# The first two units of a graph layer in halves, with the end of the setup between their products

## The reference

```python
HW = einsum('bnf,fo->bno', layernorm(x), W)
A_norm = relu((A + A.T) * 0.5)
D = sum(A_norm, axis=1);  d = D ** -0.5 where D > 0, else 0
out = relu((eye(N) - d[:, None] * A_norm * d[None, :]) @ HW)
x = x + out
x = x + moe(layernorm(x))     # 8 experts, top 2, gelu(t @ w1 + b1) @ w2 + b2
```

## Time and profile before

| | us |
|---|---|
| median of three runs | 880.55 |
| profiled execution | 878.45 |
| its span, first to last instruction | 876.3 |
| TensorE busy | 840.2 (96%) |
| DVE, ACT, POOL busy | 638.6, 476.6, 325.3 |

### The profile page before, as it was taken

One profiled execution on the slowest core, in us unless ns is written; L12 is line 12 of the kernel. 1 busy time (PEld: TensorE's weight loads), 2 busy tenths in 40 slices (PEclk: granted clock), 3 DMA queues, 4 the chain that ended last, 5 costly groups with the idle time before them and its releaser, 6 DMA issues.

```text
span 876.3 us, 14318 instructions
## 1 busy us (share of the span) xinstructions
PE 840.2 (96%) x4098; PEld 698.8 (80%) x4098; DVE 638.6 (73%) x1558; ACT 476.6 (54%) x871; POOL 325.3 (37%) x319
## 2 busy tenths in 40 slices
PE   3688999999999999999999999999999999999998
PEld 3577788888888888888888787788888888888886
DVE  3688644578889654442516499999999999999997
ACT  2687423233334200121111488888888888888886
POOL 1893253564757545455445539101000000000000
PEclk9996999999999999999999999999999999999999
DMA  9994376686766257977778866777877777777772
GB/s 282 330 318 142 120 276 253 228 288 237 267 210 211 90 178 285 327 269 263 258 277 313 307 247 231 271 286 284 296 272 266 262 265 281 275 288 292 286 267 80
DMA packets 93472, 223.00 MB, mean 254 GB/s; under 512 B 8904, under 2 KB 60128, under 8 KB 81520
## 3 DMA queue, kind: packets, MB, share of 16 engines
q1 hardware_dynamic: 88304, 213.23, 68.5%
q0 software_dynamic: 2608, 8.33, 2.4%
q10 hardware_dynamic: 2512, 0.86, 0.4%
HBM read 157.89 MB, written 64.49 MB: 254 GB/s over the span
## 4 chain that ended last, share of the span: by engine, by line
PE 90%; DVE 3%; ACT 3%; issue 2%; DMA 1%; POOL 1%; DVEq 0%; ACTq 0%; POOLq 0%
PE bank L959 13%; PE bank L961 13%; PE bank L960 13%; PE bank L1408 6%; PE bank L1392 6%; PE bank L1394 6%; PE bank L1405 6%; PE bank L1393 6%; PE bank L1406 6%; PE bank L344 3%; PE bank L448 2%; PE bank L896 2%; PE bank L1414 1%; PE bank L325 1%; ACT s_tri L607 1%
## 5 line engine op out<-in xcount | busy, mean ns | idle before, releaser
L1450 ACT ACTIVATE act_h<-bank,b_sb 128x512 f32<-128x512 f32 x256 | 176.9, 691 | 46.2 <-PE bank L1394 37.3
L1492 DVE TENSOR_TENSOR gated<-c_all,act_h 128x512 f32<-128x512 f32 x256 | 177.8, 695 | 25.1 <-ACT act_h L1450 19.7
L1497 DVE TENSOR_TENSOR g_lo<-gated,g_hi 128x512 fp32r<-128x512 f32 x256 | 175.7, 686 | 0.2
L1457 ACT ACTIVATE g_hi<-gated 128x512 fp32r<-128x512 f32 x256 | 159.6, 623 | 6.1 <-DVE gated L1492 6.0
L1368 POOL DMA_DIRECT2D out<-fin x31 | 23.7, 763 | 308.3 <-DVE fin L1505 308.3
L1030 POOL TENSOR_SCALAR z<-x,mv,rstd 128x128 f32<-128x128 f32 x128 | 107.6, 853 | 3.4
L959 PE MATMUL bank<-y_hi,stage 128*128 128x512 f32 x256 | 105.7, 413 | 1.3 <-DVE y_lo L734 0.7
L981 ACT ACTIVATE z_hl<-bank 128x512 fp32r<-128x512 f32 x32 | 19.2, 599 | 155.2 <-PE bank L896 155.2
L1392 PE MATMUL bank<-z_e,w_hi 128*128 128x512 f32 x256 | 102.7, 401 | 0.1
L1408 PE MATMUL bank<-g_lo,w_hi 128*128 128x512 f32 x256 | 100.9, 394 | 1.1 <-DVE g_lo L1497 1.0
L961 PE MATMUL bank<-y_hi,stage 128*128 128x512 f32 x256 | 101.3, 396 | 0.0
(11 more groups left out here) (133 smaller groups left out, 1487.8 us busy)
## 6 DMA issues: line engine op xcount, KB each, us to landing
c_all<-c_scratch SPq DMA_DIRECT2D x64, 1024.0 KB, 8.0
s_scratch<-stage SPq DMA_DIRECT2D x14, 2048.0 KB, 8.2
stage<-s_scratch SPq DMA_DIRECT2D x14, 2048.0 KB, 7.9
z_e<-z_scratch SPq DMA_DIRECT2D x32, 512.0 KB, 7.3
z_scratch<-z_hl SPq DMA_DIRECT2D x31, 512.0 KB, 2.7
x_raw<-in_x SPq DMA_DIRECT2D x32, 256.0 KB, 6.4
x_res<-in_x SPq DMA_DIRECT2D x32, 256.0 KB, 7.2
r_e<-res_scratch SPq DMA_DIRECT2D x32, 256.0 KB, 2.7
```

What stands on the lines that cost most here:

```text
L1450: act.activation(v.act_h[e % R][:, :], ps_h[e % 2][:, :], ACT.Gelu, bias=v.b1_sb[:, e:e + 1]).then_inc(gelu_done, 1)
L1457: act.activation(v.g_hi[e % R][:, :], v.gated[e % R][:, :], ACT.Copy).then_inc(hi_done, 1)
L1492: dve.tensor_tensor(out=v.gated[e % R][:, :], in0=v.c_all[s][:, e, :], in1=v.act_h[e % R][:, :], op=ALU.mult).then_inc(gated_done, 1)
L1497: dve.tensor_tensor(out=v.g_lo[e % R][:, :], in0=v.gated[e % R][:, :], in1=v.g_hi[e % R][:, :].bitcast(FP32), op=ALU.subtract).then_inc(lo ...
```

## The change

Units 0 and 1 are each multiplied in two parts: blocks 15 to 8 of unit 0, the same of unit 1, blocks 7 to 0 of unit 0, the same of unit 1. d comes in two parts (8 to 15, 0 to 7). Rows 3 to 0 of adj (the 13th to 16th) are transposed between the products of the first part and leave the loop over the rows. x blocks 8 to 11 go with the 8th to 11th row, and x blocks 12 to 15 are loaded behind all rows and worked on between products; two new x buffers lie where Y will be. Two groups of unit 0's S are made behind the sixth and seventh row, its direct blocks behind the eleventh. Groups of S are counted from the top block down, and products wait for the part of S that they need. The sums of the last rows use two PSUM banks instead of three. turn_z and route of units 0 and 1, and the stores of these units, move to units 2 and 3.

```diff
-    PARTS = [(8, 16), (3, 8), (0, 3)]
+    PARTS = [(8, 16), (0, 8)]
-    LAST = 6
-    FIRST_AT = {15: (0, 1), 14: (2, 3)}
-    SECOND_AT = (7, 5, 3, 0)
-    JOBS = [2, 2, 2, 2, 1, 1, 1, 1, 1, 1, 1, 1, 0, 0, 0, 0]
+    LAST = 9
+    ROWS_APART = 12
+    JOBS = [2, 2, 2, 2, 0, 0, 0, 1, 1, 1, 1, 0, 0, 0, 0, 0]
...
+        for k in range(EARLY, MB):
+            pr.load(sp, k)
...
 # scalar (ACT)
+        for r, j in enumerate(ROWS[:ROWS_APART]):
             for k in jobs(r):
                 pr.copy_x(act, k)
             for g in range(n_groups(j)):
                 relu(r, j, g)
+            for k in [k - 1 for k in jobs(r) if k] if r < 4 else [7] if r == 4 else [r] if r >= 8 else []:
+                pr.keep(act, k)
+            if r in (5, 6):
+                st.high_group(act, 0, r - 5)
+            if r == 10:
+                st.high_direct(act, 0)
+                y_high(15)
+                y_high(14)
+        y_high(13)
+        y_high(12)
+        relu(12, 3, 0)
+        y_high(11)
+        relu(13, 2, 0)
+        y_high(10)
+        relu(14, 1, 0)
+        y_high(9)
+        relu(15, 0, 0)
+        st.high_direct(act, 1)
+        st.high_group(act, 1, 0)
+        y_high(8)
+        st.high_group(act, 1, 1)
+        pr.copy_x(act, 12)
+        act.wait_ge(pr.xt_turned, EARLY)
+        act.wait_ge(pr.x_mv_done, EARLY)
+        st.high_group(act, 0, 2)
+        y_high(7)
+        pr.keep(act, 12)
+        pr.copy_x(act, 13)
+        y_high(6)
+        st.high_group(act, 1, 2)
+        pr.keep(act, 13)
+        pr.copy_x(act, 14)
+        y_high(5)
+        y_high(4)
+        st.high_group(act, 0, 3)
+        pr.keep(act, 14)
+        pr.copy_x(act, 15)
+        y_high(3)
+        st.high_group(act, 1, 3)
+        pr.keep(act, 15)
+        y_high(2)
+        y_high(1)
+        y_high(0)
...
 # vector (DVE)
+            if r in (5, 6):
+                st.low_group(dve, 0, r - 5)
+            if r == 8:
+                degrees(0)
+                for u in range(2):
+                    st.diagonal(dve, u)
             if r == 9:
+                add_columns(8)
+            if r == 10:
+                st.low_direct(dve, 0)
+                y_low(15)
+                y_low(14)
+        y_low(13)
+        y_low(12)
+        add_columns(7)
+        add(12, 3, 0)
+        y_low(11)
+        add_columns(6)
+        add(13, 2, 0)
+        y_low(10)
+        add_columns(5)
+        add(14, 1, 0)
+        y_low(9)
+        add_columns(4)
+        add(15, 0, 0)
+        st.low_direct(dve, 1)
+        st.low_group(dve, 1, 0)
+        y_low(8)
+        add_columns(3)
+        add_columns(2)
+        add_columns(1)
+        st.low_group(dve, 1, 1)
+        pr.statistics(dve, 12)
+        degrees(1)
+        st.low_group(dve, 0, 2)
+        y_low(7)
...
 # tensor, in the setup
+            if r in (4, 11):
+                pr.project(pe, 7 if r == 4 else 11)
             for g in range(n_groups(j)):
                 turn(r, j, g)
+            if r == 5:
+                st.turn_group(pe, 0, 0)
+            if r == 6:
+                st.turn_group(pe, 0, 1)
...
 # tensor, units 0 and 1
+        def after_first(u, m):
+            if u == 0 and m >= 8:
+                if m == 14:
+                    v.turn_last(12, 3, 0)
+                if m == 12:
+                    v.turn_last(13, 2, 0)
+                if m == 11:
+                    v.turn_last(14, 1, 0)
+                    st.turn_group(pe, 1, 0)
+                    st.turn_group(pe, 1, 1)
+                if m == 10:
+                    v.turn_last(15, 0, 0)
+            elif m >= 8:
+                if m == 15:
+                    pr.turn_x(pe, 12)
+                if m == 13:
+                    for k in range(7, -1, -1):
+                        v.column_sum(k)
+                if m == 12:
+                    pr.project(pe, 12)
+                    pr.turn_x(pe, 13)
+                if m == 11:
+                    st.turn_group(pe, 0, 2)
+                if m == 10:
+                    pr.project(pe, 13)
+                    pr.turn_x(pe, 14)
+                if m == 9:
+                    st.turn_group(pe, 1, 2)
+            elif u == 0:
+                if m == 7:
+                    pr.project(pe, 14)
+                    pr.turn_x(pe, 15)
+                if m == 6:
+                    st.turn_group(pe, 0, 3)
+                if m == 5:
+                    pr.project(pe, 15)
+                if m == 4:
+                    st.turn_group(pe, 1, 3)
+            else:
+                if m == 5:
+                    st.turn_group(pe, 2, 0)
+                    st.turn_group(pe, 2, 1)
+                if m == 2:
+                    st.turn_group(pe, 2, 2)
+                    st.turn_group(pe, 2, 3)
+        for part in range(4):
+            u = part % 2
+            for m in range(MB - 1, 7, -1) if part < 2 else range(7, -1, -1):
+                if u == 0:
+                    pe.wait_ge(v.y_lo_done, MB - m)
+                pe.wait_ge(st.lo_made, st.ops_for(u, m))
+                products(u, m, u, acc[u], MB - 1 - m)
+                after_first(u, m)
```

More of the change, by code:

```diff
@@ L442, in turn_group @@
     def turn_group(pe, u, g):
[L443 removed]
+        n, G = column(u), turn_index(u, g)
+        a, b = blocks(u, g)
         if G >= 2:
[L445 to L447 removed]
+            pe.wait_ge(lo_made, ops_with(*part_turned[G - 2]))
+        for m in range(a, b):
+            i = m - a
             last = pe.transpose(ps_t[G % 2][:, i * P:(i + 1) * P], v.s_tri[:, block(n, m), :], v.ident[:, :])
@@ L590, in gpsimd @@
                 add_columns(j)
-            if r == 10:
+            if r == 9:
                 root(0)
-            if r == 14:
-                root(1)
-        root(2)
+        pr.invert(pool, [EARLY])
+        root(1)
+        for k in range(EARLY + 1, MB):
+            pr.invert(pool, [k])
     def scalar(act):
@@ L834, in graph_stage @@
     each_router, each_rest = diagonal[:, :, 0:E], diagonal[:, :, E:2 * E]
+    LATE = [[], [], [0], [1, 2]] + [[u - 1] for u in range(4, U)]
     def landed(eng, sems, u):
@@ L930, in between @@
             if i == 12:
-                if u:
+                if u > 2:
                     turn_z(u - 1)
-                for g in groups[2:4] if u else ():
+                for g in groups[2:4]:
                     st.turn_group(pe, u + 1, g)
-            if u > 1 and i == ROUTE_AT:
+            if u > 3 and i == ROUTE_AT:
                 route(u - 2)
-        pe.wait_ge(v.relued, v.all_groups)
-        for u in range(U):
+            if u == 2 and i == 10:
+                turn_z(0)
+            if u == 2 and i == 14:
+                route(0)
@@ new lines, in between, with products @@
+            if u == 3 and i == 3:
+                turn_z(1)
+            if u == 3 and i == 11:
+                route(1)
+        def products(u, m, s, out, i):
+            h = half(u)
+            y_hi, y_lo = (v.y0_hi[:, m, :], v.y0_lo[:, m, :]) if h == 0 else (v.y1[m][:, 0, :], v.y1[m][:, 1, :])
+            s_hi, s_lo = v.stage[s][:, 0, m, :], v.stage[s][:, 1, m, :]
+            pe.matmul(out[:, :], s_hi, y_hi, start=(i == 0), stop=False)
+            pe.matmul(out[:, :], s_hi, y_lo, start=False, stop=False)
+            last = pe.matmul(out[:, :], s_lo, y_hi, start=False, stop=(i == MB - 1))
+            if i == MB - 1:
+                last.then_inc(acc_done, 1)
@@ L940, in tensor @@
+        for u in range(2, U):
             h = half(u)
@@ L952, in tensor @@
             for i, m in enumerate(order):
-                if u == 0:
-                    pe.wait_ge(v.y_lo_done, MB - m)
+                if h == 0:
+                    pe.wait_ge(st.lo_made, st.ops_for(u, m))
                 if u == MB:
                     pe.wait_ge(pr.y1_lo_done, m + 1)
[L957 to L963, removed]
+                products(u, m, s, out, i)
                 between(u, i + 1)
```

181 lines of the change are left out of this document (97 added, 84 removed).

## The result

The changed kernel takes 906.42 us (median of 6 executions, 905.57 to 906.76); the kernel before took 880.9 beside it (6, 878.72 to 881.92). The ratio is 1.0293 with the interval 1.0279 to 1.0308: the change costs about 25.5 us. The profiled execution took 906.75 us for a span of 904.7, 28.3 more than that of before. The forecast was 896.7 with a range up to 905: the sign was right, the loss half as large again as forecast. The first product came at 78.64, where 72.5 was forecast; later than 76 was one of the forecast's own signs that the loss would be larger.

What follows compares the result with a forecast made beforehand. TensorE bounds the kernel, so unit 2's start decides: 15.1 us later, plus 0.4 for turn_z(0) and 2.7 for the clock, 18.2 on the profiled execution's 878.45, giving 896.7 us; range 886 to 905.

Steps and rivals of the forecast that it cites:

- one of the forecast's own signs: First product after 76 us would mean the chain through rows 5 to 10 is longer than priced, the loss larger.
- the trips: Upper half of unit 0, last four rows: add, ReLU, y_high, y_low strictly one behind the other, 13.45 us in sum.
- the waits: TensorE waits before project(13), (14), (15) and block 2 of unit 0: 2.0, 0.7, 1.4 and 2.4, together 6.5 us.
- The first rival: Not slower: last four rows hide beside products, upper half done before 82.9 us means no loss; 875.3 us, 7%.
- the rows up to keep(8): Setup, x work out of rows 4 to 6, S groups in: keep(7) at 48.36, keep(8) at 62.0 us.
- up to row 4 all queues that matter stand as before: Setup up to row 4: project(7) starts at 43.17, row 4's adds run from 44.78, keep(7) to 48.36 us.
- the clock, one fall and +2.7: TensorE falls to its low rate at 91.9 us, once, for 6 us: 4.5 blocks, 0.6 each, +2.7 us.
- The third rival: Clock low again and again: half of the 26.1 us at half rate, net +8 over the sum, 904.5 us; 10%.
- the last 26.1 us of work ahead of unit 2: TensorE's work left after unit 0's block 8: 24 blocks, four x blocks, one-column passes and transposes, 26.1 us without waits.
- rows 9 and 10: Setup: keep, projection, transposes, add, ReLUs and keep one behind the other, 4.4 and 4.3 us, to 70.7 us.
- the degrees: Upper half's tiny comparison on DVE takes 0.17 us, not 1.16, without POOL's column addition; otherwise 0.6 us more.

Runs made afterwards that it cites:

- The best version: Changed kernel with two banks, y_highs and x copies earlier in ACT's queue, idle transposes in the setup and ahead of unit 0's blocks: 890.27 us.
- the kernels with two banks: Changed kernel with x blocks 9 and 11 projected into bank 3 instead of bank 5: 903.24 us.
- with y_high ahead: Changed kernel with each y_high from block 11 on one place earlier in ACT's program, ahead of a late row's ReLU: 901.34 us.
- the kernel with the copies early: Changed kernel with copies of x blocks 13 to 15 ahead of the S group and keeping before them in ACT's program: 902.55 us.
- The fillers in the setup alone: Changed kernel with idle transposes (8 to 18) behind rows 2, 3, 6, 8, 9 and 10 of the setup loop: 901.77 us.
- the kernel with all fillers: Changed kernel with the setup's idle transposes and 8 to 16 more before blocks 13, 11, 10, 9, 8, 2 of unit 0 and project(13): 899.88 us.
- the kernel with the orders and the banks: Changed kernel with two banks, y_highs of blocks 11 to 8 ahead of ReLUs, x copies 13 to 15 ahead of S groups, no filler: 896.19 us.

## Why the forecast had the sign and not the size

**Right: the trips and the waits.** Trips 13.4 us against 13.45, waits 6.9 against 6.5. Taking the serial link out of the trips shortened them by 4.4 us; taking out three of the waits, 4.5 us, gave 3.9. The first rival, no loss, needed the upper half done by 82.9. The best version has block 8 done at 87.7, with the y_highs ahead, two banks and the clock up.

**Right at full clock: the rows up to keep(8).** The forecast had keep(7) done at 48.36 and keep(8) at 62.0. A keep is done 1.0 us after its start: in the changed kernel 52.15 and 65.66. But the kernels with two banks and with y_high ahead run the same instructions as the changed one up to row 8, and in their profiled executions the clock stayed at 1.00 from 10 us to the end of keep(8): 48.44 and 61.95, 47.98 and 61.47. The keeps of the changed kernel, and below them those with y_high ahead:

```profile
51.15 1.12 ACT L367 ACTIVATE hw<-bank,x_rstd 128x128 f32<-128x128 f32 x4
...
64.66 1.11 ACT L367 ACTIVATE hw<-bank,x_rstd 128x128 f32<-128x128 f32 x4
...
46.98 1.11 ACT L367 ACTIVATE hw<-bank,x_rstd 128x128 f32<-128x128 f32 x4
...
60.47 1.12 ACT L367 ACTIVATE hw<-bank,x_rstd 128x128 f32<-128x128 f32 x4
```

So "up to row 4 all queues that matter stand as before" held for the queues, and the 3.7 us at keep(8) are the clock's. They are all lost ahead of keep(7): the kernel with the copies early, which has one low stretch before it (29.5 to 32.9) and no filler, has keep(7) done at 49.87, the changed kernel, which has two, at 52.15. From keep(7) to keep(8) it is 13.5 us in all four, with the clock low on the way (53.4 to 60.2 in the kernel with the copies early) or not. So a low clock costs what it lengthens on the path, and here nothing beside it.

**Wrong: the clock, one fall and +2.7.** This is the step that failed. The term came from one fall in the earlier trace rows, in the place where the old kernel had its waits; the forecast put it behind the upper half and priced the whole setup at the full rate, with no term for the clock there. The changed kernel has six stretches. The fillers in the setup alone gave 4.7 us (906.42 to 901.77), those behind it 1.9 more (to 899.88). So keeping the clock up behind the setup gave back 1.9, where 2.7 was forecast, and the missing term is the setup's 4.7. With the fillers in all of them (41.1 us of low clock down to 3.4) the profiled time falls from 906.75 to 899.78: the term is 7.0 or more, as the fillers may cost something themselves, not 2.7, and explains 4.3 of the 10.1 us by which the profiled execution missed the forecast. That is 0.18 us for each microsecond at the lower level, since in much of that time TensorE waits anyway. It is no fixed price: between two executions of the kernel with the orders and the banks, 896.04 us at a clock of 0.985 and 890.89 at 0.992, it is about 0.4.

The third rival, "clock low again and again", came nearest (904.5) and had 10%, but that is in part luck. It put the low clock into the last 26.1 us of work ahead of unit 2, and only some 7 of the 41.1 us lie there (98.5 to 102.2 and 126.0 to 129.5); its +8 more than the sum met 4.3 of the clock and 5.8 of small terms. The Trainium skill ("TensorE: Matmul & The Clock Gate", section "A second HAM failure mode: psum-queue depth-cycling") tells of a kernel in which frequent short idle gaps between groups of products let the clock swing over and over. The trace of the changed kernel agrees in that it swings, six times, where the rows of before had one fall. It does not agree with the place that the forecast took from the rule: ahead of projections 13 to 15 TensorE waits 2.19, 0.82 and 1.52 us, and the clock is 1.00 from 102.2 to 126.0; only the fourth wait is followed by a low stretch.

**Small terms, all on one side.** The other 5.8 us are read from the kernel with all fillers. First product at 74.31, not 72.5: +1.8. Of that, keep(8) done at 63.15, not 62.0, is 1.15; it is most likely the clock again, in the stretch at 28.9 to 32.3 that the fillers left. The rest is rows 9 and 10, which took 4.7 and 4.6 us from keep to keep (forecast 4.4 and 4.3). From the end of y_low(8), at 92.97, to unit 2 at 128.77 it is 35.8, where 33.3 was forecast: +2.5; the first product behind another kind of work starts the chain some 0.08 us later than the 0.685 for a block allows, and the waits with their fillers are 1.1 longer. From unit 2 to the end 768.9, 2.0 more than before (0.4 was forecast): +1.6, which was not explained. The median lies 2.1 above the profiled execution of before, which the forecast named and did not add.

**Right: the degrees.** 0.17 us at 64.31, not 1.16: with no column addition of POOL beside it the tiny comparison is short. The lock that the Trainium skill describes ("SBUF — State Buffer", section "Who interferes with whom") would have it so; that it was this lock is not shown.

**Still open.** Why the clock falls more often in the changed kernel. All six executions of it have a mean clock of 0.977 to 0.983, all 27 of the kernel before beside the experiments 0.987 to 0.995, so the change lowers it. The likely reason is that it takes work from TensorE in the setup and spreads gaps, but which gap brings a fall is not shown: the same instructions keep the clock up from 35 to 60 us in one execution and not in the next, with TensorE busy 6 to 7 of 10 us in both. Nor was the remaining 9 us of the best version taken apart further than this: block 8 done at 87.7 instead of 82.9, and the rest of units 0 and 1 with its x work longer than priced.

## What to carry to other kernels

Where work is spread out to start products earlier, count what it leaves TensorE to do in each stretch: gaps that cost nothing in the queues can cost clock, and the price falls on the serial path next to them. In a queue worked strictly in order, put what the next engine waits for ahead of what merely fills the time: four instructions moved ahead were worth 3 to 5 us. And count the banks of a chain that is meant to overlap: a projection that must wait for the keep of the block before it does not overlap with it. Where a clock can differ from one execution to the next, compare an edit at equal clocks: 4.3 of the 6.1 us that a second bank seemed to win were the clock's.

## What the runs showed of the hardware

Idle transposes made a kernel faster: 4.7 us with 82 of them in the setup, 6.5 with 178, the clock's mean going from 0.977 to 0.989 and 0.997. The same kernel in executions at different clocks: 904.35 us at 0.979, 900.37 at 0.989; 897.07 at 0.986, 890.89 at 0.992. In the kernel before, half of the low stretch could be taken away for a gain of 0.8 us (0.1 to 2.3). And a stretch of 6.8 us at the lower level (53.4 to 60.2, kernel with the copies early) cost nothing: keep(7) to keep(8) took 13.5 us with it and without it.
